# Attention scores stacked to 96 rows, exponentials of three units, a 24-unit ring and nine tiles summed by DMA

## The reference, cut to what matters

```python
qkv = jnp.einsum('oc,bchw->bohw', w_qkv, x)
q, k, v = split into (b, 8 heads, 32, 4096)
scores = jnp.einsum('bhdi,bhdj->bhij', q, k) / sqrt(32)
attn = jax.nn.softmax(scores, axis=-1)
out = jnp.einsum('bhij,bhdj->bhdi', attn, v)
return jnp.einsum('oc,bchw->bohw', w_proj, out) + x
```

## Time and profile before

| | |
|---|---|
| median of 3 runs | 2516.49 us (2513.29 to 2516.5) |
| profiled execution, span | 2517.7 us, 62570 instructions |
| TensorE matmul / ScalarE / VectorE busy | 97% / 90% / 86% of the span |
| DMAs issued by GpSimd | 512, 53.2% of 16 engines' span |

### The profile page before, as it was taken

How to read it: one execution, slowest core, us unless ns; L and a number is a source line. 1 busy time by engine, 2 the same in 40 slices (tenths; PEclk the granted TensorE clock), 3 DMA queues, 4 the chain that set the end, 5 groups by cost and what they waited for, 6 DMA issues and landing times.

```text
span 2517.7 us, 62570 instructions
## 1 busy us (share of the span) xinstructions
PE 2451.0 (97%) x27104; PEld 783.8 (31%) x27108; DVE 2155.3 (86%) x1386; ACT 2261.4 (90%) x2510; POOL 455.4 (18%) x652
## 2 busy tenths in 40 slices
PE   8999999999999999999999999999999999999998
PEld 3222222242222222344442222222422222223443
DVE  6899999978999999895578999999799999998954
ACT  7999999989999999666489999999899999995663
POOL 0222222202222222110012222222022222220200
PEclk9999999999999999999999999999999999999999
DMA  3777777726777777302237777777177777772011
GB/s 118 147 145 144 147 147 143 147 51 135 148 146 146 146 147 146 92 1 73 82 71 147 148 142 148 147 143 148 43 146 144 148 144 146 147 144 64 1 60 42
DMA packets 96406, 300.38 MB, mean 119 GB/s; under 512 B 18704, under 2 KB 19792, under 8 KB 95856
## 3 DMA queue, kind: packets, MB, share of 16 engines
q0 software_dynamic: 73728, 268.47, 53.2%
q1 hardware_dynamic: 22400, 27.92, 3.4%
HBM read 18.95 MB, written 8.68 MB: 11 GB/s over the span
## 4 chain that ended last, share of the span: by engine, by line
ACT 55%; PE 21%; DVE 14%; issue 6%; DMA 2%; ACTq 0%; POOL 0%; DVEq 0%; SPq 0%; POOLq 0%
ACT arena L517 36%; ACT arena L516 18%; DVE arena L561 10%; PE psOL L851 7%; PE scores L308 3%; DMA arena<-arena 2%; PE psOL L445 2%; PE psOL L775 1%; PE scores L319 1%; PE psOL L434 1%; PE scores L838 1%; PE scores L839 1%; PE scores L828 1%; PE scores L829 1%; DVE arena L1003 1%
## 5 line engine op out<-in xcount | busy, mean ns | idle before, releaser
L561 DVE TENSOR_TENSOR arena<-arena 128x2048 f32<-128x2048 f32 x704 | 1613.4, 2292 | 99.1 <-ACT arena L517 39.8
L517 ACT ACTIVATE arena<-scores 128x1536 f32<-128x1536 f32 x1024 | 1553.6, 1517 | 0.0
L445 PE MATMUL psOL<-arena 128*32 128x512 f32 (+1 forms) x11264 | 1078.9, 484 | 3.0 <-ACT arena L517 1.4
L434 PE MATMUL psOL<-arena 32*128 32x512 f16 x3072 | 835.6, 377 | 12.3 <-ACT arena L516 10.9
L434 PE MATMUL scores<-arena 32*128 32x512 f16 x9216 | 842.6, 378 | 0.0
L516 ACT ACTIVATE arena<-psOL 128x512 f32<-128x512 f32 x1024 | 669.4, 654 | 3.4 <-PE scores L434 3.4
L587 POOL DMA_DIRECT2D arena<-arena x448 | 387.6, 889 | 1136.5 <-ACT arena L517 840.8
L434 PEld LDWEIGHTS psOL<-arena 32*128 32x128 f16 x3072 | 206.3, 92 | 826.0 <-ACT arena L516 706.1
L445 PEld LDWEIGHTS psOL<-arena 128*32 128x32 f32 x11264 | 267.9, 108 | 518.7 <-issue 431.1
L434 PEld LDWEIGHTS scores<-arena 32*128 32x128 f16 x9216 | 220.0, 92 | 0.0
L851 PE MATMUL psOL<-arena 128*128 128x512 f16 x768 | 172.0, 382 | 0.0
(11 more groups left out here) (120 smaller groups left out, 1419.1 us busy)
## 6 DMA issues: line engine op xcount, KB each, us to landing
arena<-arena POOLq DMA_DIRECT2D x512, 512.0 KB, 5.3
X<-in_x SPq DMA_DIRECT2D x16, 512.0 KB, 5.3
out<-arena SPq DMA_DIRECT2D x32, 256.0 KB, 2.0
arena<-att_inv SPq DMA_DIRECT2D x16, 256.0 KB
arena<-pool_inv SPq DMA_DIRECT2D x2, 2048.0 KB, 7.1
arena<-in_w_qkv SPq DMA_DIRECT2D x1, 768.0 KB, 4.4
Ls<-L SPq DMA_DIRECT2D x32, 8.0 KB
att_inv<-Ls SPq DMA_DIRECT2D x32, 8.0 KB
```

The costliest lines, as they stand in the source:

```text
L434: last = nc.tensor.matmul(dst[h], K[rows, kp, j * 128:(j + 1) * 128], Q[rows, qp, cs], start=(n == 0), stop=(n == 2))
L445: last = nc.tensor.matmul(both[h * D:(h + 1) * D, lo:hi], V[:, j, h * D:(h + 1) * D], P[:, r + h, lo:hi], start=(j == 0), stop=(j == JT - 1))
L517: nc.scalar.activation(P[:, r + 1:r + G, :], bank[n % 2].rearrange("p (u n) -> p u n", n=CH), ACT.Exp, scale=SCORE).then_inc(s_exp, 1)
L561: nc.vector.tensor_tensor(acc[:], old, P[:, r:r + G, :], ALU.add).then_inc(s_add, 1)
```

## The change

- **Scores in the values' shape.** K is stored as `KS`, 96 rows for each head (high, high, low), and Q as `QS2`, 96 rows (high, low, high), for two chunks of queries at a time. One matmul over 96 rows and 32 columns of the array gives all three terms for 32 keys; a unit takes 4, a tile 16.
- **Stacking by SP.** The projection writes a chunk's parts into one of two buffers `staged[c % 2]`. A new `sync` of the projection moves them: 12 DMAs for K per chunk (32 rows of 1 KB each), 12 more for Q in chunks 0 and 1, and one that stores Q's parts in DRAM, 128 in all for a projection. ScalarE waits for the stacking of chunk c - 2 before it writes chunk c. The exponentials wait before unit 12 for the stacking of the last two chunks, because `staged` lies under the ring. Q for chunks 2 to 7 is loaded from DRAM by 3 DMAs each during the attention.
- **Exponentials in threes.** A group is 3 units (1536 wide), across tile boundaries; an attention has 342 groups. The scores of group k + 2 wait for the exponential of group k.
- **Ring.** 24 units, that is 6 tiles instead of 8.
- **Sums.** `SUM_D` has nine tiles; VectorE makes 22 adds of tiles instead of 23, and one add of `accD` to `acc` (`merge`) in the next chunk. There is one product with ones (`sums`) for a chunk, eight groups into the next one; for the last chunk there are two as before. `acc` is double, and the outputs of the chunks take turns in psO and psL.
- Buffers have been moved for this.

```diff
-RING = 8
-LAG = 2
-SUM_D = [2, 6, 9, 13, 16, 20, 23, 27]
+GROUP = 3
+RING = 24
+SUM_D = [4, 7, 10, 13, 16, 18, 21, 24, 26]
+def exps_through(c, j):
+    return ((c * JT + j) * G + G - 1) // GROUP + 1
+def halves_by(k):
+    if k == GROUPS - 1:
+        return 2 * NC * JT
+    halves = min(k * GROUP // 2, 2 * (min((k + 1) * GROUP, UNITS) // G))
+    return halves - (halves % (2 * JT) in (1, 2 * JT - 1))
...
+            def stacked(c):
+                return 16 * (1 + 6 * G + (1 + 3 * G) * (c // 2))
...
+                    if c >= 2:
+                        act.wait_ge(s_st[c % 2], stacked(c - 2))
+                    nc.scalar.activation(staged[c % 2][:, :, 0, :], both_units(c), ACT.Copy, scale=1.0 / WS
...
+            def sync(sp):
+                for c in range(NC):
+                    cs = slice(c * CH, (c + 1) * CH)
+                    sp.wait_ge(s_ev, c + 1)
+                    for h in range(G):
+                        heads_rows = slice(h * D, (h + 1) * D)
+                        for r, part in enumerate((0, 0, 1)):
+                            sp.dma_start(KS[r * D:(r + 1) * D, h, cs], staged[c % 2][heads_rows, 1, part, :]
+                                         ).then_inc(s_st[c % 2], 16)
+                        if c < 2:
+                            for r, part in enumerate((0, 1, 0)):
+                                sp.dma_start(QS2[c][r * D:(r + 1) * D, h, :], staged[c][heads_rows, 0, part, :]
+                                             ).then_inc(s_st[c], 16)
+                    sp.dma_start(q_dram[:, :, cs].rearrange("s p n -> p s n"), staged[c % 2][:, 0, :, :]
+                                 ).then_inc(s_st[c % 2], 16)
...
+                def scores(k):
+                    for i in range(group_size(k)):
+                        n, h = divmod(k * GROUP + i, G)
+                        c, j = divmod(n, JT)
...
+                        for m in range(4):
+                            last = nc.tensor.matmul(bank[k % 2][m * D:(m + 1) * D, i * CH:(i + 1) * CH],
+                                                    KS[0:3 * D, h, j * 128 + m * D:j * 128 + (m + 1) * D],
+                                                    QS2[c % 2][0:3 * D, h, :], start=True, stop=True)
                     last.then_inc(s_ready, 1)
...
+                for k in range(GROUPS):
+                    pe.wait_ge(s_exp, k + 1)
+                    if k + 2 < GROUPS:
+                        scores(k + 2)
...
+                    for c in range(NC - 1):
+                        if k == exps_through(c, JT - 1) + 8:
+                            sums(pe, c)
+                    at, end = halves_by(k - 1) if k else 0, halves_by(k)
...
+                for k in range(GROUPS):
+                    u, size = k * GROUP, group_size(k)
+                    act.wait_ge(s_ready, k + 1)
+                    if u == 6:
+                        act.wait_ge(s_nx, NC)
+                    if u == 12:
+                        for c in (NC - 2, NC - 1):
+                            act.wait_ge(s_st[c % 2], stacked(c))
+                    for m in range(u, u + size):
+                        if m % G == 0 and m >= RING:
+                            slot_free(act, (m - RING) // G)
+                    nc.scalar.activation(P[:, u % RING:u % RING + size, :],
+                                         bank[k % 2][:, 0:size * CH].rearrange("p (u n) -> p u n", n=CH),
                                          ACT.Exp, scale=SCORE).then_inc(s_exp, 1)
...
+            def merge(dve, c):
+                for k in range(2):
+                    dve.wait_ge(s_dma[k], 16 * len(SUM_D) * (c + 1))
+                dve.wait_ge(s_add, (c + 1) * ADDS)
+                nc.vector.tensor_tensor(acc[c % 2], acc[c % 2], accD, ALU.add).then_inc(s_merged, 1)
...
                 for c in range(NC):
-                    if c:
-                        sums_out(dve, c - 1)
                     for n in range(ADDS):
+                        if n == 1 and c:
+                            merge(dve, c - 1)
+                        if n == 6 and c:
+                            sums_out(dve, c - 1)
...
+                    project[0].sync(sp)
                     attend[0].sync(sp, b)
...
+                    project[1].sync(sp)
                     attend[1].sync(sp, b, lambda sp: layer1.signals["rows"](sp, b))
```

More of the change, by code:

```diff
@@ L406, in attention, with both, sums @@
             s_tr = sem(root, f"s_tr0_{g}")
-            lead, both = psO, psL
+            s_q = [sem(root, f"s_q{k}_{g}") for k in range(2)]
+            guard = psL
+            def both(c):
+                return (psO, psL)[c % 2]
+            def sums(pe, c):
+                pe.wait_ge(s_o_free, c + 1)
+                pe.wait_ge(s_merged, c + 1)
+                for h in range(G):
+                    last = nc.tensor.matmul(both(c)[h * D:(h + 1) * D, :], ones[:], acc[c % 2][:, h, :],
+                                            start=True, stop=True)
+                last.then_inc(s_sum, 1)
             def sums_of_acc(pe, c):
@@ L411, in sums_of_acc @@
                 for h in range(G):
-                    last = nc.tensor.matmul(both[h * D:(h + 1) * D, :], ones[:], acc[:, h, :], start=False, stop=True)
+                    last = nc.tensor.matmul(both(c)[h * D:(h + 1) * D, :], ones[:], acc[c % 2][:, h, :],
+                                            start=False, stop=True)
                 last.then_inc(s_sum, 1)
@@ L419, in sums_of_dma @@
                 for h in range(G):
-                    last = nc.tensor.matmul(both[h * D:(h + 1) * D, :], ones[:], accD[:, h, :], start=True, stop=False)
+                    last = nc.tensor.matmul(both(c)[h * D:(h + 1) * D, :], ones[:], accD[:, h, :],
+                                            start=True, stop=False)
                 last.then_inc(s_sum, 1)
             def tensor(pe, free):
-                def scores(c, j):
-                    cs = slice(c * CH, (c + 1) * CH)
-                    rest = bank[(c * JT + j) % 2]
-                    dst = [lead] + [rest[:, k * CH:(k + 1) * CH] for k in range(G - 1)]
-                    if c == 0 and j % 4 == 0:
-                        pe.wait_ge(s_ev, j // 4 + 1)
-                    for n, (kp, qp) in enumerate(TERMS):
-                        for h in range(G):
-                            rows = slice(h * D, (h + 1) * D)
-                            last = nc.tensor.matmul(dst[h], K[rows, kp, j * 128:(j + 1) * 128], Q[rows, qp, cs],
-                                                    start=(n == 0), stop=(n == 2))
-                    last.then_inc(s_ready, 1)
@@ L789, in tensor @@
                 if between:
[L790 removed]
+                    pe.wait_ge(behind.signals["exp"], GROUPS)
                 broadcast(0)
```

217 lines of the change are left out of this document (108 added, 109 removed).

## The result

The changed kernel takes 3013.07 us (median of 4 runs, 3010.72 to 3018.09), the kernel before 2516.47: a ratio of 1.1978 (1.1961 to 1.1995). It is slower by 497 us, where 230 were forecast. The profiled execution has a span of 3016.5 us against 2517.7, so 498.8 us are to be found.

A forecast was written before the change was run, and what follows sets the result against it. The prediction took TensorE (97% busy) and ScalarE (90%) as close, ScalarE setting the pace. Span 2517.7 + 166 (ring) + 64 (projections) = 2748, so 2746 us as median; by itself 2640 to 2800, with rivals 2640 to 2930.

The forecast's parts named there:

- TensorE's shape: Attention matmuls: with one array shape the gaps between scores and values go, 1.30 us a group.
- The rival of staying gaps: TensorE in the attention still pauses at each change of type: group 1.49 us, chunk 65.7, total 2800; chance 0.05.
- ScalarE's pace: Exponentials in the attention: 1.35 us a group, 57.6 us a chunk in place of 58.9, 42 us less in 32 chunks.
- the last rival: Transfers hide everywhere, in ring and stacking, leaving ScalarE's pace: 2518 - 26 = 2492 us; chance 0.06, of which 0.04 faster.
- The chunk: Attention chunk stalled by ring and accumulating DMAs: 22.8 + 7S = 64.1 us, 5.2 more than 58.9, 166 us in all.
- S = 5.9: Time the accumulating transfers need for one tile of `SUM_D`, in us; taken near the lower bound of 5.6.
- The upper bound, 6.7,: Highest transfer time a tile, read from five steps between second-half issues; would make the chunk 69.7 us, 346 us more.
- The last term, 9.9,: End of a chunk: 7.33 groups from the group waiting for tile 26 to the next tile 4, 9.9 us.
- The landing times and the reach: Ring: tiles must land within 8.1 us of their exponentials, last halves land after 9 to 12; stall at tiles 18 to 26.
- The projections: SP's 128 stacking issues at 0.37 us delay the exponentials 16 us a projection, 64 in all; bounds 31 and 186.
- the rival of long issues: SP's new stacking DMAs in the projections cost 0.63 us each, 186 us in all: total 2870; chance 0.17.
- Starved transfers: Transfers in the attention stay at 6.7 us a tile, perhaps as VectorE holds GpSimd's port: total 2928; chance 0.12.

The follow-up runs named there:

- x2: The changed kernel with K and Q stacked through DRAM, 46 DMAs of SP a projection in place of 128: 2808.23 us.
- z4: The changed kernel with stacking through DRAM and without GpSimd's accumulating transfers, so nine tiles a chunk are missing from the sums: 2498.9 us.
- y2: The kernel before with the changed kernel's nine tiles in `SUM_D`, ring still 8 tiles: 2639.55 us, ratio 1.0498.
- y3: The kernel before with the nine tiles in `SUM_D` and exponentials waiting for the tile six before instead of eight: 2717.18 us, ratio 1.0804.
- x4: The changed kernel with most of VectorE's additions cut to 128 of 512 columns, GpSimd's transfers unchanged: 3016.0 us.
- x1: The changed kernel without GpSimd's accumulating transfers, the nine tiles of `SUM_D` missing from the sums: 2701.85 us.
- z1: The changed kernel with stacking through DRAM, eight evenly spread tiles in `SUM_D`, and `accD` summed by TensorE instead of the merge: 2644.78 us, ratio 1.0515.
- x3: The changed kernel whose accumulating transfers carry one head of two, half the bytes with as many issues and waits: 2704.36 us.

## Why the forecast was right in its sign and half as large as the loss

Two of the runs divide the 498.8 us of span. x2 differs from the changed kernel in the stacking alone: 3016.5 - 2806.5 = 210.0. z4 differs from x2 in the transfers alone: 2806.5 - 2497.2 = 309.3. What remains of z4 against before, 2497.2 - 2517.7, is -20.5. They add up to 498.8. (Three chips were used; the medians of the kernel before on them lie within 1.6 us.) The forecast had 64 for the first, and for the other two together 166, where the runs show 288.8. Two steps failed: the time for which a new DMA holds SP's queue, which was the larger miss (146 us with what hangs on it), and the length of a chunk behind the ring (123 us).

**TensorE's shape: right.** 0.66 and 0.86 us for three and four rounds, no gap at a change of type. The rival of staying gaps falls with it.

**ScalarE's pace: right.** 1.343 us a group where nothing waits; the gain of 20.5 us, 16 beside the runs of its own chip, is somewhat under the 26 of the last rival, with the open point named at z4.

**The chunk: mechanism right, size off.** It was to be 12.9 to the landing of tile 7, 7S with S = 5.9, and 9.9 to the next tile 4, together 64.1. In the chunk shown, the exponential of tile 4 ended 0.29 before the issue at 312.54 (the distance of the earlier trace rows), at 312.25, and the next at 381.81. Tile 7 landed 13.2 later, at 325.4; tile 26 after (369.1 - 325.4)/7 = 6.24 a tile; then 381.8 - 369.1 = 12.7 passed. So in this chunk the first term was right within 0.3, the step S cost 7 x 0.34 = 2.4 more, and the last term 2.8 more. On average over the 28 chunks the three are 13.7, 7 x 6.23 and 11.4, together 68.7: 0.8, 2.3 and 1.5 more than forecast. So S is the largest miss of the three, and the last term of the chunk shown is above the usual.

- *S = 5.9* was to hold because waiting work would fill the engines' pauses. In the window above GpSimd's queue takes 89.6% of 43.7 us, 5.6 us a tile, which is the forecast's lower bound. SP's queue takes 3.3%, 0.2 us a tile, and some 0.4 is pause. The Q loads were in no term: they were put "at nothing" as running "on an idle SP", though what they share is the 16 engines. In the first and last chunk of an attention, where no Q is loaded, S is 6.0; in the six between it is 6.3. y2 and y3, which load no Q, have 6.04 and 6.01. That the loads make the difference is read from this and was not tested by a run of its own. That stalled exponentials deliver the next tile late and so stretch S isn't borne out: y3 stalls over twice as long as y2 (150.1 against 66.4 us in the rows shown) at the same S. It isn't VectorE either (x4).
- *The upper bound, 6.7,* was no pace of the transfers. The issues at 360.41 and 393.95 are released by exponentials and belong to tiles 9 and 27: 18 tiles of 1.84 us in five steps are 6.6. The step was ScalarE's, and not "each after the landing of the one before".
- *The last term, 9.9,* had ScalarE at its full pace behind the stall. What happened is in the timelines: TensorE idles behind ScalarE, its clock is then granted at half, its scores come late, and ScalarE waits for them. x1, without stalls, has 66 us less of such waits, 2.1 a chunk. The forecast had TensorE and VectorE "catch up" in the stall, so that their overruns come "at nothing", and no step of it had the clock fall. That the lost time is the clock's and not the refilling of the two engines' pipeline alone was not separated by a run. z1 waits 45.6 us for scores with a granted clock of 1.00 in an attention (window 110:540), so such waits arise at full clock too.

**The landing times and the reach: right.** 9 to 12 us were named, the averages of tiles 10 to 26 are 9.1 to 10.9, and in the chunk shown tile 26 took 12.5. The reach was judged rightly, but the stalls were put at tiles 18 to 26, and they begin at tile 10, whose landing after 9.6 us on average is already over 8.1.

**The projections: the step that failed most.** "What an issue holds SP for": the new DMAs were taken "as L1175, 0.37 with the gap", because of their 1 KB rows. They cost as much as L224's, 0.59 and 0.62 to 0.63 from start to start. The length of the rows, on which the choice rested, does not settle the price: the store of Q's parts takes 0.58 in a row of issues and 0.37 behind a pause, and all 32 issues of L1175 in the kernel before stand behind a pause, while those of L224 stand in a row. Yet a small move within SBUF (4 KB) is dear there even behind a pause of many us, as SP's timeline of the kernel before shows:

```profile
1117.41 0.61 SPq L1164 DMA_DIRECT2D arena<-arena  x1
```

What parts the two prices, size, direction or what stands ahead in the queue, no run separated. The upper bound of that very step, all 0.63, gave 186 us, and 210 were lost; the rival of long issues had the right price. The rest, 24 us or 6 a projection, lies in places that the step did not price: the fifth group was to be 16 us late and is some 49, 41 from the longer projection and 8 from its own wait, and how much of it is TensorE's slower clock behind these waits no run separated. The Trainium skill (DMA: Bandwidth & Descriptors, Anatomy of one DMA), with its 50 ns of dispatch, would have had the stacking nearly free; the measured 0.591 us on SP speaks against using it for this queue.

**The range.** Each of the two dear terms came out near its upper bound, and the range let only one of them do so: 186 and 346 together make 3050, over the measured 3013. The two had been treated as rivals that exclude each other, though one is SP's queue and the other the 16 engines.

**Rivals.** Long issues: held for its own term; its 2870 had the chunk at 64.1. Starved transfers: its chunk of 69.7 us was near 68.7 by luck, since the step is 6.2 and not 6.7, and the mechanism is refuted: a VectorE with 951 us more of waits leaves the step at 6.16. The Trainium skill (SBUF — State Buffer, two separate sides) ties the locked-out descriptors to VectorE operations in a two-port mode, a condition that the rival left out; x4 agrees with it in that these additions of two tensors cost the transfers nothing measurable. Gaps stay: fell. Ring wide enough, and transfers hide: fell, though x3 shows that at half the bytes they would hide from the ring.

## What to carry to other kernels

Before a buffer between an engine and its DMAs is made shorter, compare its reach in us with the landing time and the spacing of the transfers with the bytes' own time: here 8.1 us against 9 to 12, and 3.6 to 5.4 us against 6.2. Count in it every other transfer on the same engines: the Q loads were 3.3% of them. Before a step between issues is taken for the pace of the transfers, look at what releases each issue. Price a row of small DMAs as count times issue time on the issuing queue, from a row in the trace with the same size, direction and neighbours in the queue; where none matches, take the dear one. When two unrelated terms are uncertain, let the range hold both at their dear end. Behind the longest stall of the chunk shown TensorE also ran at half clock, so such a stall can cost more than its length.

## What the runs showed of the hardware

In the chunk shown, the second accumulating transfer of a tile (512 KB within SBUF) lands 4.5 us after its issue at the end of the chunk and after 5.0 to 7.1 before that, and TensorE's granted clock went to half after an idle stretch of 2.30 us, while stretches of up to 1.42 us had left it at 1.00. That VectorE added a quarter of the columns made no difference to the transfers: 6.16 against 6.20 us a tile. SP's issue time is 0.591 us for 32 partitions of 1 KB within SBUF and 0.332 for L1175, and for one and the same store of 256 KB 0.58 in a row of issues and 0.37 behind a pause. In x2, a lone store of 256 KB took 0.38 and the one behind it 0.47, and three loads with 4 rows of 1 KB for each of 32 partitions 1.76 together (its SP timeline):

```profile
601.06 0.38 SPq L417 DMA_DIRECT2D k_parts<-arena  x1
601.48 0.47 SPq L417 DMA_DIRECT2D q_parts<-arena  x1
615.36 1.76 SPq L424 DMA_DIRECT2D arena<-k_parts  x3
```
